# Gate and up of a mixture of experts from high and low parts of rows and weights, rounded on the chip, with the shared tiles split eleven and five

## What is computed

```python
def _expert(x, Wg, Wu, Wd):
    return jax.nn.silu(x @ Wg.T) * (x @ Wu.T) @ Wd.T
shared = _expert(x, Wg_s, Wu_s, Wd_s)
probs = jax.nn.sigmoid(jnp.einsum('bsh,eh->bse', x, Wr) + rb)
scores, idx = jax.lax.top_k(probs, 2)
cw = (jax.nn.one_hot(idx, 8, dtype=x.dtype) * scores[..., None]).sum(-2)
out = shared
for e in range(8):
    out = out + cw[..., e:e + 1] * _expert(x, Wg[e], Wu[e], Wd[e])
```

## Time and profile before

| | us |
|---|---|
| median of 3 runs | 1090.48 |
| lowest and highest | 1089.4, 1093.59 |
| the profiled execution | 1090.56 |
| its span | 1088.8 |
| TensorE's matmuls busy in it | 1050.0 (96%) |
| DVE busy | 657.6 |
| ACT busy | 574.5 |
| POOL busy | 201.1 |

### The profile page before, as it was taken

The page is one execution under the profiler, slowest core; times in us unless marked ns, Lnnn a source line. Parts: engine busy times, 40 slices in busy tenths (PEclk is TensorE's granted clock), DMA queues, the critical chain, the costliest instruction groups (busy, mean ns, idle before and its releaser), DMA issues. The chain is left out here.

```text
span 1088.8 us, 15032 instructions
## 1 busy us (share of the span) xinstructions
PE 1050.0 (96%) x5573; PEld 521.1 (48%) x5573; DVE 657.6 (60%) x907; ACT 574.5 (53%) x1065; POOL 201.1 (18%) x212
## 2 busy tenths in 40 slices
PE   5889999999999999999999999898999999999998
PEld 2443445444445433544434433224666666666665
DVE  3989786895687897678798588222642222222216
ACT  2138777886687777577777578762211111111111
POOL 4017400009000006300000040020011333333210
PEclk9989999999999999999999999999999999999999
DMA  6451220420211420302112100111920111111125
GB/s 170 107 156 24 42 62 1 121 61 1 61 33 29 122 48 13 62 1 60 37 26 61 41 20 2 59 58 50 368 89 25 49 39 49 49 45 44 39 71 181
DMA packets 38278, 70.11 MB, mean 64 GB/s; under 512 B 6848, under 2 KB 23360, under 8 KB 38208
## 3 DMA queue, kind: packets, MB, share of 16 engines
q1 hardware_dynamic: 30832, 56.42, 19.8%
q0 software_dynamic: 3744, 10.23, 3.0%
q10 hardware_dynamic: 3632, 2.51, 0.9%
HBM read 33.70 MB, written 9.31 MB: 40 GB/s over the span
## 5 line engine op out<-in xcount | busy, mean ns | idle before, releaser
L610 ACT ACTIVATE probs<-ring_ps 128x512 f32<-128x512 f32 (+1 forms) x832 | 443.1, 597 | 138.2 <-PE ring_ps L770 133.4
L883 DVE TENSOR_REDUCE mpart<-s_ps 128x2 f32<-128x1024 f32 x384 | 458.0, 1221 | 85.7 <-PE s_ps L757 85.7
L770 PE MATMUL ring_ps<-qst,kst 64*128 64x512 f32 (+1 forms) x832 | 233.3, 465 | 3.9 <-ACT probs L610 3.3
L785 PE MATMUL pv_ps<-probs,vp 128*32 128x512 f32 (+2 forms) x1664 | 222.3, 607 | 0.7 <-ACT probs L610 0.7
L770 PEld LDWEIGHTS ring_ps<-qst,kst 64*128 64x128 f32 (+1 forms) x832 | 100.8, 181 | 218.2 <-ACT probs L610 111.0
L757 PE MATMUL s_ps<-kst,qst 63*128 63x512 f32 (+1 forms) x1024 | 182.3, 400 | 8.3 <-DVE mpart L883 6.9
L1105 ACT ACTIVATE s_sb<-gu_ps 128x512 f32<-128x512 f32 x55 | 32.9, 597 | 256.7 <-PE gu_ps L1196 256.7
L1363 DVE TENSOR_TENSOR h_sb<-s_sb,gu_ps 128x512 f32<-128x512 f32 x55 | 37.8, 687 | 170.3 <-ACT s_sb L1105 170.2
L1196 PE MATMUL gu_ps<-wgu,xbT 128*128 x312 | 140.3, 592 | 0.0
L757 PEld LDWEIGHTS s_ps<-kst,qst 63*128 63x128 f32 x1024 | 92.2, 186 | 69.4 <-DVE mpart L883 43.7
L217 POOL TENSOR_SCALAR veps<-mv 128x4 f32<-128x4 f32 x8 | 1.9, 232 | 535.9 <-DVE mv L852 285.8
(11 more groups left out here) (183 smaller groups left out, 885.5 us busy)
## 6 DMA issues: line engine op xcount, KB each, us to landing
kst<-parts SPq DMA_DIRECT2D x45, 401.0 KB, 5.3
qst<-parts SPq DMA_DIRECT2D x48, 128.0 KB, 4.5
wgu<-in_WgT SPq DMA_DIRECT2D x16, 256.0 KB, 7.6
wgu<-in_WuT SPq DMA_DIRECT2D x16, 256.0 KB, 7.9
wd<-in_WdT SPq DMA_DIRECT2D x8, 512.0 KB, 9.7
wgu<-picked SPq DMA_DIRECT2D x8, 512.0 KB, 7.4
cold<-in_ctxT SPq DMA_DIRECT2D x3, 800.5 KB, 4.1
cold<-in_ctxT SPq DMA_DIRECT2D x6, 400.2 KB, 6.0
```

Source lines behind the costliest of these rows:

```text
L610: nc.scalar.activation(probs[0:w, m % NPB, h, :], ring_ps[0:w, bank(("st", idx)), :], ACT.Exp, scale=SCALE).then_inc(exp_done, 1)
L770: nc.tensor.matmul(ring_ps[0:w, bank(("st", idx)), :], kst[u % NKB][rows, h // 2, mt * P:mt * P + w], qst[u % NKB][rows, h // 2, :], start ...
L785: last = nc.tensor.matmul(pv_ps[32 * h:32 * h + c1 - c0, :], values[:, c0:c1], probs[0:w, m % NPB, h, :], start=(mt == 0), stop=(mt == MT ...
L883: nc.vector.tensor_reduce(mpart[:, :, p, t, q], s_ps[:, n % NSP], AX.X, ALU.max).then_inc(s_free, 1)
```

## The change

Each product of gate and up in a sorted block is made from three fp32r products: high row part by high weight part, high by low, low by high. Four fp32 products become twelve fp32r products. The low by low product is left out. The shared tiles and all down products stay fp32.

The parts are made on the chip. Rows: ACT rounds a turned block from t_ps (xb_hi, `high_block`), DVE subtracts (xb_lo, `take_block`). Weights: ACT rounds gate and up of each expert (gate_hi, up_hi: 16 instructions of 1024 columns, in turns 5, 7, 8, 9 of its loop), and the differences replace the weights in place (wgu_lo has the address of wgu): 4 on POOL (gate of experts 0 to 3), 12 on DVE (in turns 7, 8, 9). The high parts lie in memory that is dead by then: gate_hi over xn2 and hot_row, up_hi over attention's buffers, the buffers of the lists and the first nine shared tiles of xn2T. For this the buffers were moved, xn2T is laid out by tiles, and the silu is written to h_sb instead of a buffer of its own. The new waits are for these buffers to be dead, and for all 16 low parts ahead of the first block.

Eleven shared tiles lead and five end. A block is turned ahead of the gate of the job before it, and no longer behind it.

```diff
-EARLY = 9
+EARLY = 11
+FRONT = 9
...
+UNDER = E * 2 * F2 - FRONT * D
+AT_GATE, AT_UP = {5: range(0, 4), 7: range(4, 8)}, {8: range(0, 4), 9: range(4, 8)}
...
-        xn2T = parts[:, TT * D:2 * TT * D].rearrange("p (k n) -> p k n", k=2)
+        xn2T = parts[:, 0:TT * D].rearrange("p (t k n) -> p t k n", k=2, n=P)
...
+        with nc.sbuf_tensor("up_hi", [P, E, 2, F2], F32R) as up_hi:
+            pass
...
+            with nc.sbuf_tensor("gate_hi", [P, E, 2, F2], F32R) as gate_hi:
+                pass
...
+        hot_row = sb("hot_row", [P, 2, TT, P], F32R)
+        with nc.sbuf_tensor("wgu_lo", [P, E, 2, 2 * F2], F32R) as wgu_lo:
+            pass
         wgu = sb("wgu", [P, E, 2, 2 * F2])
...
             rstd_on_pool(nc, pool, LAST, mv, veps, rstd, power, ln, 1, sq, 0)
+            for e in AT_GATE[5]:
+                pool.wait_ge(gate_hi_ready, e + 1)
+                nc.gpsimd.tensor_tensor(wgu_lo[:, e, :, 0:F2], wgu[:, e, :, 0:F2], gate_hi[:, e].bitcast(F32),
+                                        ALU.subtract).then_inc(lo_ready, 1)
...
             def silu(i):
                 act.wait_ge(gu_full, i + 1)
                 if i >= 2:
-                    act.wait_ge(h_ready, i - 1)
-                nc.scalar.activation(s_sb[:, i % 2, :], gu_ps[:, i % 2, 0, :], ACT.Silu).then_inc(silu_done, 1)
+                    act.wait_ge(ht_full, i - 1)
+                nc.scalar.activation(h_sb[:, i % 2, :], gu_ps[:, i % 2, 0, :], ACT.Silu).then_inc(silu_done, 1)
+
+            def high_block(r):
+                act.wait_ge(t_full, r + 1)
+                if r >= 2:
+                    act.wait_ge(gu_full, EARLY + r - 1)
+                nc.scalar.activation(xb_hi[:, r % 2].rearrange("p k n -> p (k n)"), t_ps[:, 0:2 * P], ACT.Copy
+                                     ).then_inc(xb_hi_ready, 1)
+
+            def high_gate(e):
+                act.wait_ge(w_e[e], 80)
+                if e == 0:
+                    act.wait_ge(turned, 1)
+                    act.wait_ge(rows_stored, 16)
+                if e == 4:
+                    act.wait_ge(held_full, 1)
+                nc.scalar.activation(gate_hi[:, e], wgu[:, e, :, 0:F2], ACT.Copy).then_inc(gate_hi_ready, 1)
+
+            def high_up(e):
+                if e == 0:
+                    act.wait_ge(lists_done, 1)
+                if e == 4:
+                    act.wait_ge(gu_full, FRONT)
+                nc.scalar.activation(up_hi[:, e], wgu[:, e, :, F2:2 * F2], ACT.Copy).then_inc(up_hi_ready, 1)
...
             for i in range(JOBS + 1):
+                if 0 <= i + 1 - EARLY < NBLK:
+                    high_block(i + 1 - EARLY)
                 if i < JOBS:
                     silu(i)
...
+                for e in AT_GATE.get(i, ()):
+                    high_gate(e)
+                for e in AT_UP.get(i, ()):
+                    high_up(e)
...
                 if r == 0:
                     for e in range(E):
                         pe.wait_ge(w_e[e], 80)
+                    pe.wait_ge(lo_ready, 2 * E)
...
+                        e = bass.ds(owners[r], 1)
+                        products = []
+                        for k in range(2):
+                            hi, lo = (up_hi if f else gate_hi)[:, e, k, :], wgu_lo[:, e, k, f * F2:(f + 1) * F2]
+                            x_hi, x_lo = xb_hi[:, r % 2, k, :], xb_lo[:, r % 2, k, :]
+                            products += [(x_hi, hi), (x_hi, lo), (x_lo, hi)]
+                    for n, (x, w) in enumerate(products):
+                        last = nc.tensor.matmul(gu_ps[:, i % 2, f, :], x, w, start=(n == 0),
+                                                stop=(n == len(products) - 1))
...
+                if 0 <= i + 1 - EARLY < NBLK:
+                    turn_block(i + 1 - EARLY)
                 if i < JOBS:
                     gate_up(i)
...
-                if 0 <= i + 1 - EARLY < NBLK:
-                    turn_block(i + 1 - EARLY)
                 if i >= 2:
                     down(i - 2)
...
             def take_block(r):
-                dve.wait_ge(t_full, r + 1)
+                dve.wait_ge(xb_hi_ready, r + 1)
                 if r >= 2:
                     dve.wait_ge(gu_full, EARLY + r - 1)
-                nc.vector.tensor_copy(xbT[:, r % 2].rearrange("p k n -> p (k n)"), t_ps[:, 0:2 * P]).then_inc(xt_ready, 1)
+                nc.vector.tensor_tensor(xb_lo[:, r % 2].rearrange("p k n -> p (k n)"), t_ps[:, 0:2 * P],
+                                        xb_hi[:, r % 2].rearrange("p k n -> p (k n)").bitcast(F32), ALU.subtract
+                                        ).then_inc(xt_ready, 1)
+
+            def rest_gate(e):
+                dve.wait_ge(gate_hi_ready, e + 1)
+                nc.vector.tensor_tensor(wgu_lo[:, e, :, 0:F2], wgu[:, e, :, 0:F2], gate_hi[:, e].bitcast(F32),
+                                        ALU.subtract).then_inc(lo_ready, 1)
...
+                if 0 <= i + 1 - EARLY < NBLK:
+                    take_block(i + 1 - EARLY)
                 if i < JOBS:
                     hidden(i)
...
                 combine(i)
+                if i == 7:
+                    for e in AT_GATE[i]:
+                        rest_gate(e)
+                for e in AT_UP.get(i, ()):
+                    rest_up(e)
```

More of the change, by code:

```diff
@@ L198, in build @@
         logit = kept("logit", [P, TT, E])
-        shared = (xn2, xn2T, wgu_s, wd_s, wr, rb, logit)
-        attention(nc, I, x1, stats, mv, veps, power, rstd, tg, ident, rows_dram, parts, cold, c0_lo, shared)
-        experts(nc, I, O, x1, stats, mv, veps, power, rstd, tg, ident, rows_dram, picked_dram, shared)
+        with nc.sbuf_tensor("up_hi", [P, E, 2, F2], F32R) as up_hi:
+            pass
+        with ExitStack() as layer:
+            halves = Halves(nc, layer)
+        with ExitStack() as layer:
+            lists = Lists(nc, layer)
@@ new lines, in build @@
+        kept("under", [P, UNDER])
+        with nc.sbuf_tensor("front", [P, PARTS - TT * D], F32):
+            with nc.sbuf_tensor("gate_hi", [P, E, 2, F2], F32R) as gate_hi:
+                pass
+        parts = kept("parts", [P, PARTS])
+        xn2T = parts[:, 0:TT * D].rearrange("p (t k n) -> p t k n", k=2, n=P)
+        xn2 = parts[:, PARTS - TT * D:PARTS].rearrange("p (t d) -> p t d", d=D)
+        shared = (xn2, xn2T, wgu_s, wd_s, wr, rb, logit)
+        attention(nc, I, x1, stats, mv, veps, power, rstd, tg, ident, rows_dram, parts, cold, c0_lo, shared, halves)
@@ new lines, in build, with __init__, sb @@
+        experts(nc, I, O, x1, stats, mv, veps, power, rstd, tg, ident, rows_dram, picked_dram, shared, lists,
+                gate_hi, up_hi)
+class Halves:
+    def __init__(self, nc, layer):
+        def sb(name, shape, dt=F32):
+            return layer.enter_context(nc.sbuf_tensor(name, shape, dt))
+        self.wq = sb("wq", [P, 2, D])
+        with nc.sbuf_tensor("w_rest", [P, 4 * D], F32R) as rest:
+            self.w_rest = rest
+        self.w_kv = sb("w_kv", [P, 4 * D])
+        self.c0_hi, self.c1_both = sb("c0_hi", [P, MP], F32R), sb("c1_both", [P, MP], F32R)
+        self.wk0_hi, self.wv0_hi = sb("wk0_hi", [P, D], F32R), sb("wv0_hi", [P, D], F32R)
+        self.wk1_twice, self.wv1_twice = sb("wk1_twice", [P, D], F32R), sb("wv1_twice", [P, D], F32R)
@@ L222, in attention @@
 def attention(nc, I, x1, stats, mv, veps, power, rstd, tg, ident, rows_dram,
-              parts, cold, c0_lo, shared):
+              parts, cold, c0_lo, shared, halves):
     xn2, xn2T, wgu_s, wd_s, wr, rb, logit = shared
@@ L274, in attention @@
         gates = sb("gates", [P, 2])
-        wq = sb("wq", [P, 2, D])
-        with nc.sbuf_tensor("w_rest", [P, 4 * D], F32R) as w_rest:
-            wk0_lo, wv0_lo, wk1_lo, wv1_lo = (w_rest[:, i * D:(i + 1) * D] for i in range(4))
-        w_kv = sb("w_kv", [P, 4 * D])
-        wk0, wv0, wk1, wv1 = (w_kv[:, i * D:(i + 1) * D] for i in range(4))
+        wq = halves.wq
+        wk0_lo, wv0_lo, wk1_lo, wv1_lo = (halves.w_rest[:, i * D:(i + 1) * D] for i in range(4))
+        wk0, wv0, wk1, wv1 = (halves.w_kv[:, i * D:(i + 1) * D] for i in range(4))
         bq, bk, b1 = sb("bq", [P, 2]), sb("bk", [P, 2]), sb("b1", [P, F1 // P])
@@ L968, in _, with experts @@
                 do(job)
-def experts(nc, I, O, x1, stats, mv, veps, power, rstd, tg, ident, rows_dram, picked_dram, shared):
+def experts(nc, I, O, x1, stats, mv, veps, power, rstd, tg, ident, rows_dram, picked_dram, shared, lists,
+            gate_hi, up_hi):
     xn2, xn2T, wgu_s, wd_s, wr, rb, logit = shared
@@ new lines, in experts @@
+        owner, token, target = sb("owner", [P, NBLK], I32), sb("token", [P, NBLK], I32), sb("target", [P, NBLK], I32)
+        hot_blk, in_blk, lower, ones = lists.hot_blk, lists.in_blk, lists.lower, lists.ones
+        count_i, count_f, thr, rows_f = lists.count_i, lists.count_f, lists.thr, lists.rows_f
+        tri_i, tri, prob = lists.tri_i, lists.tri, lists.prob
```

(9 more changed lines are left out.)

102 lines of the change are left out of this document (49 added, 53 removed).

## The result

The changed kernel takes 1080.79 us (median of 8 runs, 1077.7 to 1086.02) against 1092.06 us of the kernel before in the same rounds: a ratio of 0.9904 (95% interval 0.9884 to 0.9925). It is faster, by 11 us and not by the 19.75 forecast, and its time lies 0.8 us above the end of the range, 1080. The profiled execution took 1079.5 us with a span of 1077.7.

The account below looks back on a forecast made before the run. TensorE, never idle in the sorted blocks, was taken to bound the kernel there. The terms -25.0 - 0.75 + 1.9 + 4.1 = -19.75 us, from 1090.56, gave 1070.8, stated as 1071 us, range 1062 to 1080.

Parts of the forecast that it names:

- Gate and up: Sorted blocks: twelve fp32r products at 0.233 us each, a block 5.82 to 5.18 us, 25.0 us less over 39.
- TensorE's queue: Per block, reading the owner and its check (0.6 us) stays hidden behind the gate half (1.4 us), costing nothing.
- Owner list: First needed in job 10 instead of job 8, so job 8's gate takes 3.44 us, not 4.18: 0.75 us less.
- Rounding the weights: Before the blocks: ACT's high parts 1.03 us each, DVE's low parts 1.13, POOL's four 2.3; DVE decides, 1.9 us more.
- first rival: POOL's subtractions hold up DVE's one-hot rows, so TensorE stands 6 us: 1077, or 1079 with longer low clock; chance 0.27.
- VectorE late at block 1: TensorE's turn of block 1 waits for DVE's low part of the first block's rows: 1.9 us more, bounds 0 and 4.
- The end: Last gate's end to span end: 15.3 us instead of 11.2, combining two turns later; 4.1 us more, bounds 3 and 6.

Follow-up runs that it names:

- experiment 1: Changed kernel plus one wait: GpSimd starts its four weight subtractions only after VectorE's one-hot rows; 1074.75 us, ratio 0.9827.
- experiment 2: Changed kernel with GpSimd's subtractions deleted; VectorE makes those four low parts itself in turn 6; 1073.23 us, ratio 0.9832.
- experiment 3: Changed kernel with GpSimd's four subtractions replaced by twelve memsets that only write, those low parts left out; 1077.29 us, one run.
- experiment 4: Changed kernel with GpSimd's four subtractions replaced by multiplications by zero reading one tile, those low parts left out; 1076.89 us, one run.
- experiment 5: Kernel of experiment 2 without VectorE's up low parts of experts 4 to 7, GpSimd writing zeros instead; 1071.98 us, ratio 0.9845.
- experiment 8: Kernel of experiment 6 with VectorE's last two up low parts behind the first block's own, wait split; 1072.49 us, again 1069.5 us (ratio 0.9792).
- experiment 6: Kernel of experiment 2 with the four combines one turn earlier; 1071.32 us, ratio 0.9821; again on another chip 1072.39 us, 0.9827.
- experiment 7: Kernel of experiment 2 with ten shared tiles leading and six ending; 1076.44 us, ratio 0.9869.

## Why the prediction was wrong

- **Gate and up**: right. 0.233 forecast, 0.23 measured, 5.15 us a block instead of 5.18. The step from narrower fp32r products to 512 columns held. The rule of the Trainium skill (TensorE: Matmul & The Clock Gate, "Wait — 56ns, not 53.3ns?"), N ÷ 2.4 GHz plus about 2.5 ns, would have given 0.216; the measurement decides.
- **TensorE's queue**: right, no hole between gate and up. **Owner list**: right.
- **Rounding the weights**: this step failed. It put GpSimd's parts at "2.3 us each, about 791 to 801" and entered nothing for them in the sum. GpSimd alone takes 2.32 us each (experiment 1), so the size was right; that they are hidden was wrong. They held up four of VectorE's one-hot operations by 7.5 us in all, and at TensorE the lists and the gate behind them took 6.8 us longer: 5.1 us of lateness and 1.7 of clock. The prediction had this as its first rival, at the right place and near the right size ("It would stand for 6 us"; it counted six of VectorE's operations from 792.55 and left out the one at 791.14, the first to be caught), and gave it 0.27. Against it stood that no row showed such a pair, and "if DVE wins each turn", for which no row spoke. For it stood the overlap in time, two SBUF operands on both engines, and the rule of the Trainium skill (SBUF — State Buffer, "Who interferes with whom") that such a pair excludes each other, which this trace bears out. Weighed so, the rival's 1077, or 1079 with the longer low clock, was the better forecast.
- **VectorE late at block 1**: right, 1.9 us forecast and 1.87 found; ACT 0.97 us each (1.03 estimated), VectorE 1.13.
- **Missing**: what a wait costs behind its end. The 0.4 us of hand-over and the 1.4 us of half clock in the first block stood in no term and no bound. With them the sum closes: 1070.8 + 6.8 + 0.4 + 1.4 = 1079.4, where the profiled execution took 1079.5. That it closes to 0.1 us is partly luck: the blocks gained 0.7 us more than forecast, the tail cost 0.2 more, and 0.5 us has no place. It also holds for these two profiles only.
- **The end**: right, 15.3 forecast and 15.5 found.
- **The range** ended at 1080, the first rival's number plus 1. With that rival's chance and this unpriced wait behind it, it should have ended near 1082.

That the overlap of the two engines cost what it did is shown by experiments 1 and 2, and that it needs GpSimd's reads by 3 and 4, with one profile each. That the wait at the first block comes from VectorE's row of subtractions is shown by 5 and 8. Open stays when the clock falls behind such a wait. Behind one of 1.7 us it fell in six profiles (the changed kernel, experiments 2, 3 and 4 and both of 6) and did not in the changed kernel's second. Behind the longer one of 2.55 us in experiment 1 it did not fall either, nor behind the 1.8 and 1.9 us of experiment 8; in experiment 7 it fell. It is also open why the timed gain of several variants is smaller than their stage's, by up to about 5 us.

## What to carry to other kernels

Before work goes to an idle engine, list what its neighbour does in those microseconds, and with how many SBUF operands. Here VectorE's operations with two SBUF operands and GpSimd's subtractions took turns as if on one engine. Prefer an idle stretch of the engine that would be held up anyway: here 4.6 us fitted into VectorE's 6.5. When work is late for the first use of something, split the wait by what each product really reads, since a block's first half can hide the second half's inputs. And time the end by itself: a row of 3.25 us groups at the end can start a turn earlier, even if the first of them then waits for its data.

## What the runs showed of the hardware that I had not expected

- **GpSimd's indirect DMAs lengthen beside VectorE's subtractions.** Issuing one takes 0.94 to 0.96 us alone, as in the kernel before, but 1.84 to 1.99 us for three of them in the changed kernel, which ran beside VectorE's subtractions. In experiment 7 one was issued in the first of four subtractions of 1.13 us in a row (VectorE from 823.45 for 4.61 us) and ended 0.8 us after the last:

```profile
816.66 0.95 POOL L1132 DMA_INDIRECT xb<-rows,token  x1 [0.30 <-issue]
...
823.85 5.04 POOL L1132 DMA_INDIRECT xb<-rows,token  x1 [4.23 <-PE t_ps L1251]
```

It cost nothing here: rows are gathered four blocks ahead, and TensorE has no wait for them.
- **A tiny operation can be caught too.** In experiment 1 a VectorE operation on 39 columns with a single SBUF input took 1.14 us instead of 0.18, while GpSimd's last subtraction (until 811.56) ran:

```profile
810.48 1.14 DVE L1432 TENSOR_SCALAR second<-held 128x39 f32<-128x39 f32 x1
```

The Trainium skill (SBUF — State Buffer, "Who interferes with whom") says that a `tensor_scalar` can enter a mode that also takes the ports shared with GpSimd, and then one of the two waits for the other. The row agrees, though no run here shows in which mode it ran.
- **The same wait of 1.7 us can cost nothing or 1.3 to 1.6 us of clock behind it**, from one execution to the next, so a difference of under 2 us between two single profiles says nothing until the clock of both is laid side by side.
